# Eight linear-attention layers rewritten: centred weights, the residual added by TensorE, split f32r products, unrolled

## The chip, the cores and the metric

The kernel runs on one core of one Trainium2 chip. The metric is the time of one execution in device microseconds. All inputs are float32; the whole network is one launch.

## The reference, cut to what matters

The program chains six parts over an activation x of 4 sequences of 512 tokens with 128 features: a mixture of experts with 8 experts (A), a stack of eight linear-attention layers (B), part A again, an attention part with 4 experts (C), a state-space part (D), and C again. Only B is changed. Its input is the normalized x, and its output is added to x. One layer, with H = 16 heads of DH = 8 features and F = 512:

```python
def _phi(t):
    return jax.nn.elu(t) + 1.0

def layer(h, p):
    q = _phi((h @ wq + bq_).reshape(b, s, H, DH))
    k = _phi((h @ wk + bk_).reshape(b, s, H, DH))
    v = (h @ wv + bv_).reshape(b, s, H, DH)
    kv = jnp.einsum('bshd,bshm->bhdm', k, v)
    z = 1.0 / (jnp.einsum('bshd,bhd->bsh', q, k.sum(axis=1)) + 1e-06)
    att = jnp.einsum('bshd,bhdm,bsh->bshm', q, kv, z).reshape(b, s, d)
    h = h + att @ wo + bo_
    h = _ln(h, g1_, be1_)
    y = jax.nn.gelu(h @ w1 + c1_, approximate=False) @ w2 + c2_
    return (_ln(h + y, g2_, be2_), None)
```

After eight layers a last normalization with its own scale and shift follows, `_ln(h, gf, bef)`. `_ln` subtracts the mean over the 128 features and divides by the root of the variance.

## The kernel before

The activation lies with features on the 128 partitions and tokens along the free dimension, as four tiles of 128x512, one per sequence (batch b). Every engine has its own instruction list, written out by hand in program order, and waits on named semaphores; there is no planner. PSUM has 8 banks of 128x512.

Stage B is `pe_layers` (L646), `act_layers` (L719), `dve_layers` (L750) and `sp_layers` (L805); GpSimd (POOL) has no work in it. On each engine a loop of four iterations holds two layers, one for each half of the weight buffer `wslot`. SyncE loads the 901.5 KB of a layer's weights when the layer two before it has been left.

One layer goes so. Queries (L657): one fp32 product per batch, exponential and relu on ACT (L729, L730), minimum and sum on DVE (L761). Keys and values (L664): products of 256 columns for each 128 tokens, bias added by DVE (L774, L775), exponential and relu on ACT (L734, L735), DVE again (L767). DVE takes keys(b-2) after the bias of batch b, so keys lag by two batches. Then k times v with an extra column for the sum of keys (L672), masked by head on DVE (L784, L785), the denominators (L678), `rz` with the small constant on ACT (L737), its reciprocal on DVE (L788), the numerator product (L684) copied by ACT (L740), the spread of the reciprocal over heads (L688), the multiplication (L792), and the output projection (L692). DVE adds bias and residual (L796).

A normalization is `pe_ln`, `act_ln` and `dve_ln`: a mean product (L225, a matrix of 1/128), DVE subtracts it (L248), ACT squares (L234), a second mean product gives the variance (L228), ACT takes the logarithm (L242) and the exponential of minus half of it (L238), and DVE scales (L260) and shifts (L253). The feed-forward part has 16 fp32 products for 4 batches and 4 chunks of 128 hidden features (L701), 16 gelus (L746), 16 products back (L708), and DVE's bias and residual add (L801). PE issues ff1(b) and then ff2(b-1). A second normalization ends the layer. ACT loads its table for gelu before the first gelu, and the table with logarithm and exponential for each normalization.

The expert stages, which aren't changed, already split an fp32 operand into a high part in the type f32r and a low part, the difference, and add three products, high by high, low by high and high by low: L440, L441 and L442. There the weights' high part is a cast on DVE (L543) and the low part a subtraction on POOL (L526). Their hidden tiles are rounded by ACT (L495) and subtracted by DVE (L548). POOL also adds expert outputs (L519). In the state-space part DVE does a scan (L1439) and POOL a product (L1456).

Of the kernel before, what the change touches and what calls it, by code (L numbers as in the profile page):

```python
# [28 lines left out]
B_WQ, B_WKV, B_WO, B_W1, B_W2, B_KVB, B_VEC = 0, 128, 384, 512, 1024, 1536, 1792  # L29
B_BQ, B_BO, B_C1, B_C2, B_G1, B_BE1, B_G2, B_BE2, B_COLS = (B_VEC + i for i in (0, 1, 2, 6, 7, 8, 9, 10, 11))  # L30
# [8 lines left out]
    ("b_bc", 1), ("w_dt", DT_RANK), ("b_dt", 1), ("w_dtp", P), ("b_dtp", 1), ("a_log", NSTATE), ("dcoef", 1),  # L39
]  # L40

CONSTS = [("ident", P), ("mean", P), ("block", P), ("head_sum", 32), ("head_spread", P),
# [12 lines left out]
def build(nc, x_in, pack_a, pack_b, pack_c, params, consts, out, stages="ABACDC"):  # L55
    par_at, par_cols = columns(PARAMS)
    con_at, con_cols = columns(CONSTS)
    with ExitStack() as ctx:
# [47 lines left out]
        def view16(at, *shape):  # L106
# [30 lines left out]
        kv_bd, ks_h = view(10368, NB, P), view(10880, NB, 32)  # L137
        hid_b = view(11392, 2, FC, SEQ)
        k_exp, k_relu = view(0, NB, TPB, P), view(2048, NB, TPB, P)
        rz, att = view(0, SEQ), view(2048, NB, SEQ)  # L140
# [33 lines left out]
            gated_ok added gv_mm silu_ok q_mm q_act qf_ok kv_mm kv_ok k_act kf_ok kvs_mm kvbd_ok den_mm  # L174
            den_ok att_mm num_ok rz_ok z_bc att_ok o_mm res1_ok ff1_mm gelu_ok ff2_mm res2_ok x_ok conv_all
# [4 lines left out]
            a_exp a_ok diag_ok rows_clear bb_mm b_free cb_mm cc_ok da_ok scan_ok  # L180
# [10 lines left out]
        for kind in stages:  # L191
# [9 lines left out]
            elif kind == "B":  # L201
                count["ln"] += 2 + 2 * LAYERS
                count["lns"] += 1 + 2 * LAYERS
                count["w"] += LAYERS
                count["x_upd"] += 1
# [438 lines left out]
        ATT_BANK = [5, 6, 7, 4]  # L644

        def pe_layers(pe, c):  # L646
            n0 = c["ln"] + 1
            with pe.Fori(0, LAYERS // 2) as r:
                l = 2 * r
                for s in range(2):  # L650
                    m = 4 * (l + s)
                    w = wslot[:, s, :]
                    nd = n0 + 2 * (l + s)
                    pe.wait_ge(S[f"w_in{s}"], w_count(c, l))
                    for b in range(NB):
                        pe.wait_ge(S["ln_out"], 4 * nd - 4 + b + 1)
                        pe.matmul(ps[:, b, :], w[:, B_WQ:B_WQ + P], ha[:, b, :], start=True,  # L657
                                  stop=True).then_inc(S["q_mm"], 1)
                    for b in range(NB):
                        bank = 4 + 2 * (b % 2)  # L660
                        if b >= 2:
                            pe.wait_ge(S["kv_ok"], m + b - 2 + 1)
# [87 lines left out]
        def dve_layers(dve, c):  # L750
            n0, m0 = c["ln"] + 1, c["lns"]
            with dve.Fori(0, LAYERS // 2) as r:
                l = 2 * r
                for s in range(2):
# [15 lines left out]
                    for b in range(NB):  # L770
# [6 lines left out]
                        if b >= 2:  # L777
                            keys(b - 2)
# [948 lines left out]
```

## Time and profile before

| | us |
|---|---|
| median of 3 runs | 2228.36 (2226.25 to 2234.08) |
| the profiled execution | 2234.25 |
| its span, first to last instruction | 2232.5 |
| PE busy in the span | 1889.7 (85%) |
| DVE busy | 1437.7 (64%) |
| ACT busy | 1330.7 (60%) |
| POOL busy | 533.2 (24%) |

Times are microseconds, a count is written with x. PE is the matrix engine, PEld its weight load; a product of fp32 operands is recorded as two instructions. The granted clock of PE is a share of full speed: 1.00 is 2.4 GHz, 0.50 is 1.2 GHz. The mean over the span was 0.929. Lines of a view name the kernel's line, the engine, the operation, and the output and input tensors; `arena` is a large buffer that many tensors share. A duration is from the start of an instruction to its end, so it holds the time in which the instruction stands for a port or in a pipeline, and instructions of one engine can overlap a little.

### The profile page before, as it was taken

The page shows a single profiled execution, that of the slowest core. Times are in us where ns is not written, and L with a number is a line of the kernel's source. Part 1 is how long each engine was busy: PE and PEld are TensorE (multiplying, and loading weights), DVE is VectorE, ACT ScalarE, POOL GpSimd, SP SyncE. Part 2 cuts the span into 40 slices and gives each one's busy share as a digit, 9 for nine tenths or more (in the row PEclk, how much of TensorE's full clock was granted, in tenths as well). Part 3 has the DMA queues.
Part 4 walks back from the last instruction along what each step waited for, and adds up shares of the span by engine and source line. Part 5 has one row for each costly group of instructions (what it writes and reads, how often), then busy time and mean ns, then how long its engine had stood idle before and what let it go on. Part 6 is the DMA issues. An engine that isn't in the chain of part 4 may idle for free.

```text
span 2232.5 us, 23751 instructions
## 1 busy us (share of the span) xinstructions
PE 1889.7 (85%) x8305; PEld 1065.8 (48%) x8324; DVE 1437.7 (64%) x2318; ACT 1330.7 (60%) x2118; POOL 533.2 (24%) x525
## 2 busy tenths in 40 slices
PE   8899999999999989899677777997677677777998
PEld 6687444444434437686223233784122222332686
DVE  6687554465445646786755563786899755653787
ACT  6698646465555558797355556555654545565554
POOL 1344000000000001444411113122499501113121
PEclk9899999999999999899779998998799868999899
DMA  2431000000000003321000000210000000000110
GB/s 72 81 76 51 15 17 17 0 17 17 17 0 17 9 10 57 69 69 44 1 1 1 1 1 1 72 34 0 9 4 30 1 1 1 1 1 1 48 57 19
DMA packets 60610, 52.39 MB, mean 23 GB/s; under 512 B 2336, under 2 KB 55968, under 8 KB 60512
## 3 DMA queue, kind: packets, MB, share of 16 engines
q1 hardware_dynamic: 60512, 51.12, 8.9%
q8 instruction: 57, 0.93, 0.2%
q14 instruction: 41, 0.34, 0.1%
HBM read 49.47 MB, written 1.64 MB: 23 GB/s over the span
## 4 chain that ended last, share of the span: by engine, by line
PE 54%; DVE 22%; ACT 15%; issue 5%; DMA 2%; POOL 1%; SPq 0%; ACTq 0%; DVEq 0%; POOLq 0%
PE ps L440 8%; PE ps L442 8%; PE ps L441 8%; PE ps L708 5%; DVE arena L1439 4%; PE ps L225 4%; DVE arena L1184 4%; PE ps L701 4%; PE ps L927 3%; ACT arena L1047 2%; PE ps L897 2%; ACT rstd L242 2%; ACT arena L997 2%; ACT rstd L238 2%; PE ps L886 2%
## 5 line engine op out<-in xcount | busy, mean ns | idle before, releaser
L548 DVE TENSOR_TENSOR hid_lo<-arena,hid_hi 128x512 fp32r<-128x512 f32 x384 | 340.0, 897 | 72.2 <-ACT arena L498 70.2
L1184 DVE TENSOR_REDUCE arena<-ps 128x1 f32<-128x512 f32 (+3 forms) x352 | 214.0, 639 | 90.2 <-PE ps L901 87.4
L526 POOL TENSOR_TENSOR w_lo<-wslot,w_hi 128x512 fp32r<-128x512 f32 x56 | 76.7, 1374 | 787.8 <-DVE w_hi L543 787.8
L1104 POOL TENSOR_SCALAR_AFFINE_SELECT arena<-arena 128x256 f32<-128x256 f32 x256 | 102.5, 406 | 465.4 <-ACT arena L1047 462.8
L440 PE MATMUL ps<-x_hi,w_hi 128*128 128x512 f32 x512 | 208.7, 408 | 2.9 <-POOL w_lo L526 2.2
L441 PE MATMUL ps<-x_lo,w_hi 128*128 128x512 f32 x512 | 205.5, 401 | 0.0
L442 PE MATMUL ps<-x_hi,w_lo 128*128 128x512 f32 x512 | 205.2, 401 | 0.0
L495 ACT ACTIVATE hid_hi<-ps,wslot 128x512 fp32r<-128x512 f32 x256 | 177.1, 692 | 44.9 <-PE ps L442 17.7
L1047 ACT ACTIVATE arena<-ps 128x1024 f32<-128x1024 f32 (+3 forms) x256 | 166.3, 705 | 46.6 <-PE ps L917 45.9
L897 PE MATMUL ps<-arena 128*128 128x128 bf16 (+3 forms) x498 | 134.2, 336 | 63.5 <-DVE arena L1184 35.8
L498 ACT ACTIVATE arena<-ps,wslot 128x512 f32<-128x512 f32 x256 | 175.1, 684 | 16.8 <-DVE hid_lo L548 16.8
L440 PE MATMUL ps<-hid_hi,w_hi 128*128 128x512 f32 x384 | 153.4, 400 | 20.5 <-DVE hid_lo L548 20.5
L997 ACT ACTIVATE arena<-ps 128x1024 bf16<-128x1024 bf16 x64 | 65.4, 1021 | 151.0 <-PE ps L886 150.9
L442 PE MATMUL ps<-hid_hi,w_lo 128*128 128x512 f32 x384 | 152.9, 398 | 0.0
L441 PE MATMUL ps<-hid_lo,w_hi 128*128 128x512 f32 x384 | 151.8, 395 | 0.0
L1456 POOL TENSOR_TENSOR arena<-arena 128x512 f32<-128x512 f32 x64 | 136.1, 2165 | 45.8 <-ACT arena L1381 45.8
L519 POOL TENSOR_TENSOR x<-x,arena 128x512 f32<-128x512 f32 x64 | 108.2, 1694 | 149.6 <-DVE arena L510 149.6
L611 ACT ACTIVATE arena<-ps 128x512 f32<-128x512 f32 x128 | 76.3, 596 | 110.6 <-PE ps L442 110.5
L234 ACT ACTIVATE sq<-xc 128x512 f32<-128x512 f32 x92 | 57.6, 630 | 141.1 <-DVE xc L248 141.0
L801 DVE SCALAR_TENSOR_TENSOR res<-ps,wslot,hb 128x512 f32<-128x512 f32 x32 | 24.0, 751 | 182.7 <-PE ps L708 182.7
L701 PE MATMUL ps<-hb,wslot 128*128 128x512 f32 x256 | 116.7, 599 | 10.1 <-ACT arena L746 5.6
L746 ACT ACTIVATE arena<-ps,wslot 128x512 f32<-128x512 f32 x128 | 83.6, 690 | 67.7 <-PE ps L701 67.3
(223 smaller groups left out, 3876.7 us busy)
## 6 DMA issues: line engine op xcount, KB each, us to landing
arena<-gates_dram SPq DMA_DIRECT2D x96, 256.0 KB, 5.1
wslot<-pack_a SPq DMA_DIRECT2D x16, 514.5 KB, 3.6
wslot<-pack_b SPq DMA_DIRECT2D x8, 901.5 KB, 4.6
wslot<-pack_c SPq DMA_DIRECT2D x8, 768.0 KB, 4.6
res<-x_in SPq DMA_DIRECT2D x4, 256.0 KB, 4.4
out_dram<-res SPq DMA_DIRECT2D x4, 256.0 KB, 2.8
bc_dram<-arena SPq DMA_DIRECT2D x1, 384.0 KB, 3.2
arena<-bc_dram SPq DMA_DIRECT2D x16, 24.0 KB
```

The source lines that it names most:

```text
L440: pe.matmul(ps[:, bank, :], w1, hi, start=start, stop=False)
L441: pe.matmul(ps[:, bank, :], w1, lo, start=False, stop=False)
L442: return pe.matmul(ps[:, bank, :], w2, hi, start=False, stop=stop)
L495: act.activation(hid_hi[item % 2][:, k, :], ps[:, k, :], ACT.Gelu, bias=bias)
L498: act.activation(hid32[:, k, :], ps[:, k, :], ACT.Gelu, bias=bias).then_inc(S["hi_ok"], 1)
L548: dve.tensor_tensor(hid_lo[item % 2][:, k, :], hid32[:, k, :], hid_hi[item % 2][:, k, :].bitcast(F32), ALU.subtract).then_inc(S["hid_ok"], 1)
L701: pe.matmul(ps[:, k, :], w[:, B_W1 + k * P:B_W1 + (k + 1) * P], hb[:, b, :], start=True, stop=True).then_inc(S["ff1_mm"], 1)
L708: mm = pe.matmul(ps[:, 4 + b, :], w[:, B_W2 + k * P:B_W2 + (k + 1) * P], hid_b[:, b % 2, k, :], start=(k == 0), stop=(k == FC - 1))
L897: pe.matmul(ps[:, bank, m * keys:(m + 1) * keys], qt_s[h % 2][:, h // 2, i * P:(i + 1) * P], kt_s[b % 2][:, h // 2, 0:keys], start=(m == 0 ...
L1047: act.activation(pt[:, u % NPT, :, 0:n], ps[:, 2 * r:2 * r + 2, 0:n], ACT.Exp, scale=SCALE).then_inc(S["exp_ok"], 1)
L1184: dve.tensor_reduce(neg_max[:, i, heads[0]:heads[-1] + 1:step], ps[:, bank, 0:len(heads) * keys].rearrange("p (m k) -> p m k", k=keys), AX ...
L1456: pool.tensor_tensor(ch[:, s, t, :], hst[:, s, t, :], c_s[:, u % 2, :], ALU.mult).then_inc(S["ch_ok"], 1)
```

## The change

For each layer, and in program order:

- DVE prepares the next layer's weights during the feed-forward part: it sums the 128 output columns of Wo and of the four blocks of W2 (a reduction over 640 columns), subtracts the mean (one operation of 640 columns), and casts 640 columns (Wq, W1) and 512 columns (W2) to f32r. POOL subtracts to get the low parts.
- The constant `cent`, identity minus 1/128, is multiplied by the high and low parts of h on PE, into the same PSUM bank as the projection with the centred weights. So the bank holds the centred sum of residual and projection, and there is no mean product and no residual add. The bias, centred once for all layers, is given with the square and with the scaling.
- `kv_bd` is transposed and multiplied by the centred Wo on PE, copied back by ACT, and the queries are multiplied by the spread reciprocal before one product with it. The product of the numerator, and its copy, go. Denominators are packed into 256 columns in place of 512.
- Queries, ff1 and ff2 use three f32r products. ACT writes the high part of each normalized tile with an Identity operation; the low part is a subtraction on DVE for the middle of the layer and on POOL for h. The gelu's output is written in fp32 by ACT, copied to f32r by DVE, and subtracted on POOL; each ff2 chunk waits for both.
- ff1 and ff2 alternate by chunk, with three banks for ff1. The second normalization of batches 0 to 2 stands within and right behind the feed-forward part; that of batch 3 between the queries of the next layer. The keys(b) operation follows keys_values(b) with less lag.
- The loops are unrolled. The ACT table with logarithm and exponential is loaded once per layer, by hand, behind the gelus.

The diff, cut to its core:

```diff
 def pe_layers(pe, c):
+    def split3(bank, w_at, s, hi, lo, lo_ready, stop, start=False):
+        w1, w2 = (t[s][:, w_at:w_at + P] for t in (wb_hi, w_lo))
+        pe.matmul(ps[:, bank, :], w1, hi, start=start, stop=False)
+        pe.matmul(ps[:, bank, :], w2, hi, start=False, stop=False)
+        lo_ready()
+        return pe.matmul(ps[:, bank, :], w1, lo, start=False, stop=stop)
+    def centred(bank, hi, lo, stop):
+        pe.matmul(ps[:, bank, :], cent_r[:, :], hi, start=True, stop=False)
+        return pe.matmul(ps[:, bank, :], cent_r[:, :], lo, start=False, stop=stop)
-    with pe.Fori(0, LAYERS // 2) as r:
+    for l in range(LAYERS):
+        pe.wait_ge(S["w_parts"], c["parts"] + 2 * l + 2)
+        queries(0)
+        if l:
+            last_var(j1 - 1)
+        keys_values(0); queries(1); queries(2); keys_values(1)
+        queries(3); keys_values(2); keys_values(3)
...
+        for b in range(NB):
+            pe.wait_ge(S["g_ok"], m + b + 1)
+            centred(b, h_hi[:, b, :], h_lo[:, b, :], False)
+        pe.wait_ge(S["rz_ok"], l + 1)
...
+            pe.wait_ge(S["qz_ok"], m + b + 1)
+            pe.matmul(ps[:, b, :], kv_bd[:, b, :], qf[:, b, :], start=False, stop=True)
+        for b in range(NB):
+            var(j1, b, 4 + b)
...
+        def ff2(b, k):
+            if k == 0:
+                centred(4 + b, mid_hi[:, b, :], mid_lo[:, b, :], False)
+            pe.wait_ge(S["gelu_hi"], 16 * l + FC * b + k + 1)
+            mm = split3(4 + b, B_W2 + k * P, s, hb_b[b % 2][:, k, :], lb_b[b % 2][:, k, :],
+                        lambda: pe.wait_ge(S["gelu_lo"], 16 * l + FC * b + k + 1), k == FC - 1)
+        for item in range(NB + 1):
+            for k in range(FC):
+                if item < NB: ff1(item, k)
+                if item: ff2(item - 1, k)
...
 def act_layers(act, c):
+        queries(0)
+        if l: root(j1 - 1, 3, LN2_BANK[3])
+        queries(1)
+        if l: high(j1 - 1, 3, h_hi, ...)
+        queries(2); keys(0); queries(3); keys(1); keys(2); keys(3)
...
+        for b in range(NB):
+            root(j1, b, 4 + b)
+            if b: high(j1, b - 1, mid_hi, g1, be1, S["mid_hi_ok"])
...
 def dve_layers(dve, c):
+        queries(0)
+        if l: scaled(j1 - 1, 3, ...); shifted(j1 - 1, 3, ...)
+        queries(1); keys_values(0); queries(2); keys(0); keys_values(1)
+        queries(3); keys(1); keys_values(2); keys(2); keys_values(3); keys(3)
...
+                dve.wait_ge(S["gelu_ok"], n + 1)
+                dve.tensor_copy(hb_b[b % 2][:, k, :], hid_g[:, b % 2, k, :]).then_inc(S["gelu_hi"], 1)
+                if l + 1 < LAYERS and b in (1, 2) and k in (1, 3):
+                    weights(l + 1, 2 * (b - 1) + k // 2)
...
+def pool_layers(pool, c):
+            for b in range(NB):
+                low(l, b)                       # h_lo = ha - h_hi
+            for b in range(NB):
+                for k in range(FC):
+                    pool.wait_ge(S["gelu_hi"], 16 * l + FC * b + k + 1)
+                    pool.tensor_tensor(lb_b[b % 2][:, k, :], hid_g[:, b % 2, k, :],
+                                       hb_b[b % 2][:, k, :].bitcast(F32), ALU.subtract)
+                    if l + 1 < LAYERS and b == 3 and k in (0, 2):
+                        weights(l + 1, k // 2)
```

## Rows read from the trace of the kernel before

**Rows 1.** Busy time by stretch: stretch, length, PE, PEld, DVE, ACT, POOL, PEclk, DMA, GB/s.
```profile
232.20:813.30 581.10, 540.56 (x1601) 259.61 (x1601) 306.23 (x487) 330.74 (x514) 0.00 (x0) 1.00 0.03 11
```
**Rows 2.** Chain that ended last, parts of one layer: start, duration, what.
```profile
610.29 2.95 PE ps L672 x24
...
615.58 3.36 DVE arena L788
...
620.88 3.70 PE ps L692 x8
...
635.67 0.70 ACT arena L746
...
650.41 3.43 PE ps L701 x8
...
660.71 3.45 PE ps L225 x8
```
**Rows 3.** Timeline of PE: f32r products at half and at full clock; start, duration.
```profile
1399.33 0.63 PE L440 MATMUL ps<-x_hi,w_hi 128*128 128x512 f32 x1
1399.75 0.63 PE L441 MATMUL ps<-x_lo,w_hi 128*128 128x512 f32 x1
...
1403.18 0.39 PE L440 MATMUL ps<-x_hi,w_hi 128*128 128x512 f32 x1
1403.41 0.39 PE L441 MATMUL ps<-x_lo,w_hi 128*128 128x512 f32 x1
```
**Rows 4.** Timeline of ACT: logarithms of two batches with two operations between them.
```profile
837.80 0.67 ACT L279 ACTIVATE rstd<-ps,con 128x512 f32<-128x512 f32 x1
...
839.55 0.67 ACT L279 ACTIVATE rstd<-ps,con 128x512 f32<-128x512 f32 x1
```
**Rows 5.** Timeline of DVE and of POOL, in two stages where both work.
```profile
146.17 0.69 DVE L548 TENSOR_TENSOR hid_lo<-arena,hid_hi 128x512 fp32r<-128x512 f32 x1
146.78 1.52 DVE L543 CAST w_hi<-wslot 128x512 fp32r<-128x512 f32 x1
...
148.88 1.33 DVE L548 TENSOR_TENSOR hid_lo<-arena,hid_hi 128x512 fp32r<-128x512 f32 x1
...
146.31 1.71 POOL L526 TENSOR_TENSOR w_lo<-wslot,w_hi 128x512 fp32r<-128x512 f32 x1 [2.43 <-DVE w_hi L543]
148.38 1.29 POOL L526 TENSOR_TENSOR w_lo<-wslot,w_hi 128x512 fp32r<-128x512 f32 x1 [0.36 <-DVE w_hi L543]
...
1618.04 23.66 POOL L1456 TENSOR_TENSOR arena<-arena 128x512 f32<-128x512 f32 x11
```
**Rows 6.** Timeline of one layer: keys and values on PE, DVE and ACT.
```profile
600.24 3.62 PE L664 MATMUL ps<-wslot,ha 128*128 128x256 f32 x16
...
606.55 0.69 DVE L774 TENSOR_TENSOR arena<-ps,wslot 128x512 f32<-128x512 f32 x1 [0.89 <-PE ps L664]
...
608.41 0.61 ACT L735 ACTIVATE arena<-arena 128x512 f32<-128x512 f32 x1
...
609.55 1.99 DVE L767 SCALAR_TENSOR_TENSOR arena<-arena 128x512 f32<-128x512 f32 x3
```
**Rows 7.** Busy time by stretch, two in the attention stage, one in the state-space stage.
```profile
1197.20:1200.60 3.40, 1.69 (x16) 0.58 (x16) 0.00 (x0) 3.10 (x6) 1.48 (x4) 0.95 0.00 0
1207.20:1213.50 6.30, 5.17 (x36) 2.79 (x34) 1.79 (x6) 4.86 (x9) 1.31 (x4) 0.50 0.00 0
1620.00:1640.00 20.00, 14.41 (x37) 4.73 (x38) 20.00 (x19) 9.83 (x13) 20.00 (x11) 1.00 0.01 4
```
**Rows 8.** Timeline at the two ends of stage B.
```profile
232.16 4.84 PE L657 MATMUL ps<-ha,wslot 128*128 128x512 f32 x8
...
235.78 0.07 DVE L1611 MEMSET arena<- 128x16 f32 x1
...
826.15 2.49 DVE L1617 TENSOR_TENSOR x<-x,hb 128x512 f32<-128x512 f32 x4
```

More of the change, by code:

```diff
@@ L201, in build @@
             elif kind == "B":
-                count["ln"] += 2 + 2 * LAYERS
-                count["lns"] += 1 + 2 * LAYERS
+                count["ln"] += 1
                 count["w"] += LAYERS
+                count["parts"] += 2 * LAYERS
                 count["x_upd"] += 1
@@ L805, in sp_layers @@
[L805 to L816 removed]
+            n0 = 4 * c["ln"]
@@ new lines, in final_add, with weights, low @@
+        def final_add(dve, b):
+            dve.wait_ge(S["mid_hi_ok"], 4 * LAYERS + b + 1)
+            dve.tensor_tensor(x[:, b, :], x[:, b, :], hb[:, b, :], ALU.add).then_inc(S["x_ok"], 1)
+        def pool_layers(pool, c):
+            n0 = 4 * c["ln"]
+            def weights(l, cut):
+                s, (a, b) = l % 2, CUTS[cut]
+                pool.wait_ge(S["w_hi_ok"], c["parts"] + 2 * l + cut + 1)
+                pool.tensor_tensor(w_lo[s][:, a:b], wslot[:, s, a:b], wb_hi[s][:, a:b].bitcast(F32),
+                                   ALU.subtract).then_inc(S["w_parts"], 1)
+            def low(l, b):
+                if l:
+                    pool.wait_ge(S["h_ok"], 4 * l - 4 + b + 1)
+                else:
+                    pool.wait_ge(S["ln_out"], n0 + b + 1)
+                pool.wait_ge(S["h_hi_ok"], 4 * l + b + 1)
+                pool.tensor_tensor(h_lo[:, b, :], ha[:, b, :], h_hi[:, b, :].bitcast(F32),
+                                   ALU.subtract).then_inc(S["h_lo_ok"], 1)
+            for cut in range(2):
+                weights(0, cut)
+            for l in range(LAYERS):
+                for b in range(NB):
+                    low(l, b)
+                for b in range(NB):
+                    for k in range(FC):
+                        pool.wait_ge(S["gelu_hi"], 16 * l + FC * b + k + 1)
+                        pool.tensor_tensor(lb_b[b % 2][:, k, :], hid_g[:, b % 2, k, :],
+                                           hb_b[b % 2][:, k, :].bitcast(F32), ALU.subtract).then_inc(S["gelu_lo"], 1)
+                        if l + 1 < LAYERS and b == 3 and k in (0, 2):
+                            weights(l + 1, k // 2)
+            for b in range(NB):
+                low(LAYERS, b)
@@ L823, in build @@
+        def sp_layers(sp, c, slot_free):
+            for l in range(LAYERS):
+                s = l % 2
+                if l < 2:
+                    slot_free(sp, s)
+                else:
+                    sp.wait_ge(S["h_hi_ok"], 4 * l)
+                    sp.wait_ge(S["h_ok"], 4 * l - 4)
+                sp.dma_start(wslot[:, s, 0:B_COLS], pack_b[l]).then_inc(S[f"w_in{s}"], 16)
         SCALE = DH ** -0.5
@@ L1535, in _ @@
                     pe_layers(pe, c)
-                    last = n + 2 * LAYERS
-                    pe_ln(pe, last + 1, ha, lambda pe, t: pe.wait_ge(S["ln_out"], 4 * last + t + 1))
                 elif kind == "C":
@@ L1557, in _ @@
                     pool_experts(pool, c, x, EXPERTS0, A_PIECES, GATE_LAG0)
+                elif kind == "B":
+                    pool_layers(pool, c)
                 elif kind == "C":
```

492 lines of the change are left out of this document (316 added, 176 removed).

## The prediction

> **What bounds the kernel now.** I read the table by stretches first: the eight layers take 581.1 us of the 2232.5 us span, 72.64 us each, with PE busy 540.6 us, the granted clock at 1.00 throughout and POOL unused [rows 1]. So PE is nearly full, and removing PE work looks attractive: but the end of a layer is set by a chain, which I read next. One layer of it, with these marks [rows 2]: the first output-projection product runs to 621.74 (start 620.88 plus a quarter of 3.70); the first gelu starts at 635.67; the second feed-forward products end at 660.71; the k-times-v products end at 613.24, that is 685.88 one layer later; the next first projection ends 694.38. Four sections then make the layer: A, projection to gelu, 13.9; B, gelu to end of feed-forward, 25.0; C, that end to the end of the key-value products, 25.2; D, denominators, reciprocal, spread, first projection, 8.5. Sum 72.6. Within B the chain stands on PE all the time; in C and D it changes between ACT, DVE and PE.
>
> **What the change takes from PE.** An fp32 product of 512 columns is two passes of 0.43 us (8 passes in 3.43 us, the x8 rows) [rows 2]. An f32r product costs 0.23 at full clock and 0.43 at half [rows 3]. Three of them are 0.69 against 0.86. Per layer: 32 feed-forward products save 5.4, 4 queries 0.7, the 8 mean products 6.9, the 4 numerator products 3.4; added are 16 centring products, 3.7, and small transposes and weight products, about 1.3. PE falls from 67.6 to about 56 us. None of this is worth anything by itself; it must be followed through the sections.
>
> **Section A.** The mean product, DVE's subtraction and the residual add go (the centred sum stands in PSUM); squares start right behind the projections. The four variances wait for the last projection, so the first is there 3.6 us after the mark. Then ACT: logarithm and exponential take 1.24 per batch; with the new fourth operation (the high part) in between, 1.75, as the row pair in an expert stage shows [rows 4]. First exponential at 4.9, then three turns of 1.75 to 10.2, the last high part waiting for DVE's scaling to 11.1, table load 1.3: gelu starts 12.4 after the mark. A is 12.4, a gain of 1.5. The other table load, hidden in D before, goes at no gain.
>
> **Section B.** Each of 16 gelu tiles is now copied by DVE (f32r high part) and subtracted by POOL (low part), before the three ff2 products. The rows show how these two work beside each other: a POOL subtraction alone takes 1.29 us, beside a DVE operation that started first 1.71. A DVE cast that needs about 0.43 takes 1.52 when it meets a POOL operation: begun at 146.78, it ends at 148.30, 0.28 behind POOL's end at 148.02; a DVE subtraction takes 1.33 for the same reason; and a scan and a POOL product run alternately, 11 POOL products in 23.66, 2.15 each [rows 5]. So cast and subtraction take turns: 1.29 + 0.28 + 0.08 = 1.65 per tile when the cast waits each time, 1.17 + 0.28 = 1.45 when POOL is always queued (1.17 is 148.02 minus the DVE end 146.86). I take 1.55. B is then 1.2 (gelu 0.7, cast 0.4), 15 x 1.55 + 1.3 = 24.6, the next layer's weights, and the last ff2 product 0.4. Weights: POOL splits 640 and 512 columns, 1.46 + 1.17; DVE's centring operation of 640 columns and two casts hold POOL for 0.7 + 0.35 + 0.3, its three shifts for 0.3 each: 4.9, of which I count 4.4, since a cast fits ahead of a POOL weight operation. B comes to 30.6, a loss of 5.6. PE has 24.3 us of work in this section after the first three products, so it isn't the bound. Bounds: 28.5 at 1.45, 32.5 at 1.65, 40 if the turn is the 2.15 of the scan row, 27 if POOL never waits (then PE at 24.3 plus start and end). A gelu-table Square might force loads between gelus: four of 1.28 a layer, in ACT time that is only one third used here; zero to 5, I take zero.
>
> The Trainium skill (SBUF — State Buffer, "Who interferes with whom") says that DVE in a two-port mode, or with two SBUF inputs, and a GpSimd operation that reads SBUF exclude each other: the one that issues first keeps the pair for its whole instruction. The 1.52 and 1.33 rows agree [rows 5]. Without that rule one would add only POOL's own 16 operations, and B would be the 27 of the last bound.
>
> **Section C.** The normalization of batches 0 to 2 is now done under the feed-forward tail; only batch 3 is late, and it is passed by the next queries. The cost is a new tail: POOL's low part of h (1.3) stands behind its last gelu subtraction, so queries(0) end 1.3 after the mark, last variance 2.1, keys/values(0) 3.95 (8 passes of 3.62/16 = 0.23 [rows 6]). ACT does queries(0), root(3), queries(1), high(3), queries(2) in that order; DVE comes to keys/values(0) at 6.7. From there DVE and ACT hand each key batch back and forth. Before, the order lagged keys by two batches; now keys(1), kv(2), keys(2), kv(3), keys(3) follow without lag. One such turn is read from batch 2 of before: DVE starts at 606.55, ACT ends 608.41 + 0.61 = 609.02, and a DVE operation takes 0.68 more (1.99 for three, overlapping): 3.15 us [rows 6]. I follow it: kv(1) ends 11.1, keys(1) 13.1, kv(2) 14.3, keys(2) 16.25, kv(3) 17.45, keys(3) 19.45, the products of batch 3 end 20.6. C falls from 25.2 to 20.6, a gain of 4.6. Bounds: 17 if PE alone set it, 22 if DVE meets POOL's four low parts each time.
>
> **Section D.** Masks and transpose 1.1, denominators 0.5, reciprocal of half the columns 1.75 for 3.35 [rows 2], spread and multiply 2.0, projection 0.9, the PE queue's centring ahead of the spread 0.6: 6.9, a gain of 1.6. Bounds 6 and 8.
>
> Sum: 12.4 + 30.6 + 20.6 + 6.9 = 70.5, before the clock.
>
> **The clock.** PE has new holes. In C it has nothing from 15.1 to 16.3 and from 17.3 to 19.5 after the mark; in A it does three split products and then waits 3.4 us for the first gelu; at B's end it waits for POOL between single tiles. The rows: in 3.40 us with PE busy 1.69 the clock began to fall (mean 0.95), and 6.30 us behind another hole of that attention stage ran wholly at 0.50; where PE works 14.4 of 20 us in short regular pieces it kept 1.00 [rows 7]. The hole in C is sparser than the first of these. I expect a fall there in nearly every layer; at half clock the key-value, denominator, centring and projection products double, of which 1 to 4 us are on the chain: 2.3. In A the four tiles of lead absorb most: 0.5. At B's end the fall comes only sometimes: 0.7. Total 3.5, bounds 0 and 8. The layer is 74.0, against 72.64: plus 1.4.
>
> **Ends of the stage.** Before layer 0 the weights are split with nothing to hide it: LN done 235.8, DVE reduce, centre, two casts to 238.4, POOL 239.9 and 241.1, low part 242.4, while the queries started at 232.16 before [rows 8]. At half clock, after that wait, the keys/values of batch 0 then reach DVE at 249.2, the first projection ends about 271 instead of 258.2: plus 13 (bounds 8 and 15). Seven full layers follow: 7 x 1.4 = 9.8. The last A and B are 12.4 + 30.6 + 0.5 for 38.9: plus 4.6. The closing normalization starts from a finished centred sum; after the last ff2 product I count 16.3 + 1.2 for the clock, against 22.6 (x complete at 828.6 [rows 8]): minus 5. Loads of weights stay hidden, their DMA being asked for a full section B ahead. Unrolling is taken at nothing: the loop's branches aren't on the chain with more than issue time of a few tenths, so at most 0.5 us a layer is to be had; a price for fetching the longer code is in no row, and the unrolled expert stages show none on their chain.
>
> Sum: 13 + 9.8 + 4.6 - 5 = plus 22.4. The profiled execution took 2234.25 us (span 2232.5), 6 above the median 2228.4 of the three runs; plus 22 on the median gives 2250 us, slower by 1.0%.
>
> **The rivals.**
> 1. *The clock stays at 1.00.* Place: sections C and A; price 3.5 a layer, 4 at the start. For it: all layers now show 1.00 [rows 1]. Against: their gaps are below 1 us. It gives 9 - 7 x 2.1 + 4 - 6 = -8: 2220 us, not slower. It decides if the hole before the last key-value product leaves the clock alone.
> 2. *POOL isn't in the way.* If casts get ahead of POOL and their waits fall between its operations, B is 27.5, bounded by PE, and the layer with clock costs 71: 13 - 11.5 + 1.5 - 5 = -2; with the full clock as well, -32: 2226 and 2196. The point at which it turns: a tile turn under about 1.4 us. Against: the 1.52 cast.
> 3. *POOL's turn is 2.15, as beside the scan.* B is 9 longer in eight layers: plus 94, 2322 us. For it: [rows 5]; against: the scan holds DVE far longer than a cast.
>
> **How the numbers follow.** Forecast 0.45; rival 1 0.2; rival 2 0.17 (both parts); rival 3 0.06; 0.12 for milder mixtures on either side. Less than 0.3% (7 us) from 2228 is what a measurement of this kernel can't tell from no change. The forecast's own range is 2232 to 2280, almost all of it slower. Rival 1 is half in "faster", rival 2 half clearly faster, mixtures half: faster 0.33, same 0.12, slower 0.55. The range takes in rival 1, most of rival 2 and the upper unknowns without rival 3: 2195 to 2300.
>
> **What would show it.** The gelu subtractions on POOL should come every 1.45 to 1.65 us, filling the feed-forward stretch, with DVE casts of over 1 us; B should be 28 to 33 us. Keys of the last batch should end about 19.5 us after the last ff2 product, in turns of 3.15. The clock should show pieces at 0.50 around the key-value products. Queries of layer 0 should start near 242. Subtractions faster than 1.4, a head below 19, or a clock of 1.00 in all layers would make the prediction wrong on the side of faster; gelu table loads within the feed-forward part, on the other.

## The result, and the profile after

The changed kernel took 2259.56 us (median of 4 runs, 2258.0 to 2263.28) beside 2228.69 us for the kernel before on the same chip: a ratio of 1.0138, 95% interval 1.0115 to 1.0160. It is slower by 31 us; the forecast was 22 more, 2250. Its profiled execution took 2258.0 us with a span of 2256.3, 23.8 above the 2232.5 of before. The traces thus show 24 of the 31 us: the profiled execution of the kernel before lay 5.6 above the median of its runs, that of the changed kernel 1.6 below.

The first view is the table by stretches of the changed kernel: first the stage from its first product to its last feed-forward product (the stretch that answers to [rows 1]), then sections B, C, D and A of the layer around 600 us. Sections run here from start to start of the four marks: first output-projection product, first gelu, last feed-forward product, last key-value product. Columns: stretch, length, busy time of PE, PEld, DVE, ACT, POOL, granted clock, DMA share, GB/s.

```profile
238.16:833.41 595.25, 499.01 (x2048) 338.89 (x2048) 394.11 (x544) 361.25 (x592) 245.68 (x174) 0.95 0.03 11
584.03:612.64 28.61, 26.48 (x100) 19.78 (x100) 23.47 (x24) 18.08 (x28) 25.94 (x19) 0.94 0.00 1
612.64:633.40 20.76, 15.81 (x80) 12.52 (x80) 14.79 (x27) 13.32 (x23) 5.31 (x4) 1.00 0.13 46
633.40:644.67 11.27, 10.53 (x55) 5.34 (x52) 2.94 (x5) 2.48 (x9) 0.00 (x0) 0.85 0.00 0
644.67:658.69 14.02, 9.75 (x25) 4.48 (x25) 9.23 (x15) 11.90 (x18) 0.00 (x0) 1.00 0.00 0
```

PE was relieved as meant, from 540.6 us busy in 581 to 499.0 in 595, part of that at a lower clock; DVE now has 394 us and POOL 246. The same marks give these means over the seven layers from one first output-projection product to the next. B is 26.95 in the last layer, which has no next weights to split, and D is 11.9 in the first. (The expectations below take means over all eight layers, B 28.4 and D 10.9.)

| section, us | before | after | difference | forecast without clock |
|---|---|---|---|---|
| A | 14.8 | 14.0 | -0.8 | -1.5 |
| B | 24.45 | 28.6 | +4.2 | +5.6 |
| C | 25.4 | 20.8 | -4.6 | -4.6 |
| D | 7.9 | 10.8 | +2.9 | -1.6 |
| clock | | (in the rows above) | | +3.5 |
| a layer | 72.57 | 74.24 | +1.67 | +1.4 |

The second view is the chain that ended last, parts of one layer [rows 2]: start, duration, what.

```profile
612.55 1.49 POOL h_lo L1037
...
625.40 0.69 DVE arena L953
...
628.51 0.69 DVE arena L953
...
631.61 0.70 DVE arena L953
632.36 1.16 PE ps L721 x8
633.64 0.99 PE ps L731 x2
634.63 0.85 PE ps L732 x2
...
637.65 0.55 PE ps L731 x2
638.20 0.43 PE ps L732 x2
...
644.67 3.70 PE ps L752 x8
```

Two things are to be seen. Keys follow each other in turns of 3.11 (625.40, 628.51, 631.61), the 3.15 read from [rows 6]. And behind the key-value products PE itself is the chain: for each of four batches a product of the denominators in two halves (L731, L732), two passes each, with a transposition ahead of each (L729). At full clock that is 0.55 + 0.43 + 0.26 = 1.24 a batch, nearly 5 us in all.

The third view is the timeline of POOL and DVE in section B of that layer, which answers to [rows 5].

```profile
586.91 10.39 POOL L1048 TENSOR_TENSOR lb_b<-arena,hb_b 128x512 fp32r<-128x512 f32 x7 [0.36 <-DVE hb_b L1003]
...
605.50 1.76 POOL L1028 TENSOR_TENSOR w_lo<-wslot,wb_hi 128x640 fp32r<-128x640 f32 x1
607.22 2.70 POOL L1048 TENSOR_TENSOR lb_b<-arena,hb_b 128x512 fp32r<-128x512 f32 x2
609.88 1.30 POOL L1028 TENSOR_TENSOR w_lo<-wslot,wb_hi 128x512 fp32r<-128x512 f32 x1
611.13 1.47 POOL L1048 TENSOR_TENSOR lb_b<-arena,hb_b 128x512 fp32r<-128x512 f32 x1
```
```profile
584.75 0.43 DVE L1003 CAST hb_b<-arena 128x512 fp32r<-128x512 f32 x1 [1.10 <-ACT arena L873]
...
596.08 1.84 DVE L1003 CAST hb_b<-arena 128x512 fp32r<-128x512 f32 x2
597.83 1.58 DVE L916 CAST wb_hi<-wslot 128x640 fp32r<-128x640 f32 x1
```

The first cast, with POOL idle, takes 0.43. The other casts of this stretch take between 0.41 and 1.52 (mean over the stage 0.996), and the subtractions start 1.44 apart (median of the steps; seven end within 10.39). POOL has no gap longer than 0.4 us up to its last operation; the last feed-forward product starts at 612.64, as that ends. This is the turn that the prediction took from the 1.52 row. The Trainium skill (SBUF — State Buffer, "Who interferes with whom") has the same rule, one of the two holding the shared ports for its whole instruction; the casts of 0.43 beside an idle POOL and of up to 1.52 beside a busy one agree with it.

The rest is three pairs of rows. PE at the border of A and B; DVE and PE at the start of the stage; DVE's last additions to x.

```profile
584.77 0.50 PE L661 MATMUL ps<-mid_hi,w_hi 128*128 128x512 f32 x1 [3.67 <-ACT arena L873]
...
586.31 0.63 PE L664 MATMUL ps<-mid_lo,w_hi 128*128 128x512 f32 x1
```
```profile
235.36 1.56 DVE L929 CAST cent_r<-con 128x128 fp32r<-128x128 f32 x1
...
238.16 0.77 PE L661 MATMUL ps<-h_hi,w_hi 128*128 128x512 f32 x1 [8.80 <-POOL w_lo L1028]
```
```profile
849.80 0.69 DVE L1020 TENSOR_TENSOR x<-x,hb 128x512 f32<-128x512 f32 x1
...
851.74 0.69 DVE L1020 TENSOR_TENSOR x<-x,hb 128x512 f32<-128x512 f32 x1
```

PE waits 3.67 us for the first gelu; some eight of its next products then run at a clock of 0.50. This is so in seven of the eight layers; layer 1 kept 1.00 throughout section B. At the start a cast of 128 columns took 1.56 beside POOL. From the last feed-forward product to the last addition to x there are 21.8 us, against 23.4 before [rows 8].

The balance of the two spans: the stage is entered 2.8 earlier (DVE's last step of the first normalization starts at 232.30 for 235.12, in code that wasn't changed); from there to the first output-projection product 17.5 more; seven layer periods 11.7 more; the last A and B 1.7 more; the closing 1.6 less; what follows 2.85 less, in code that wasn't changed. Sum 23.7, of 23.8. The unchanged part after the stage took 1394.6 to 1405.2 us in the profiled executions of the twelve kernels that have the changed stage, so a few us there mean nothing.

### The profile page after: what moved, and what is told of

Read it like the earlier page. It is cut to its first block, busy times and chain, and to the rows that moved or that the text cites. A ratio compares the mean times of both kernels' runs of the same rounds, so it can differ in the third digit from the quotient of the medians.

```text
span 2256.3 us, 24548 instructions
## 1 busy us (share of the span) xinstructions
PE 1849.1 (82%) x8774; PEld 1141.6 (51%) x8774; DVE 1527.1 (68%) x2377; ACT 1372.2 (61%) x2213; POOL 786.6 (35%) x705
## 4 chain that ended last, share of the span: by engine, by line
PE 48%; DVE 25%; ACT 14%; issue 6%; POOL 4%; DMA 3%; SPq 0%; POOLq 0%; DVEq 0%; ACTq 0%
PE ps L449 7%; PE ps L451 7%; PE ps L450 7%; DVE arena L1682 4%; DVE arena L1427 4%; PE ps L1170 3%; PE ps L1140 3%; ACT arena L1290 2%; ACT arena L1240 2%; PE ps L234 2%; PE ps L1129 2%; DVE hb_b L1003 2%; PE ps L1160 1%; POOL lb_b L1048 1%; DMA arena<-gates_dram 1%
## 5 line engine op out<-in xcount | busy, mean ns | idle before, releaser
L1048 POOL TENSOR_TENSOR lb_b<-arena,hb_b 128x512 fp32r<-128x512 f32 x128 | 182.7, 1450 | 324.4 <-DVE hb_b L1003 324.4
L1140 PE MATMUL ps<-arena 128*128 128x512 bf16 (+3 forms) x512 | 139.5, 339 | 63.6 <-DVE arena L1427 34.5
L1003 DVE CAST hb_b<-arena 128x512 fp32r<-128x512 f32 x128 | 123.9, 996 | 30.2 <-ACT arena L873 29.7
L1140 PEld LDWEIGHTS ps<-arena 128*128 128x128 bf16 x512 | 43.0, 102 | 161.5 <-DVE arena L1427 99.8
```

The costliest lines, as they stand in the source:

```text
L1003: dve.tensor_copy(hb_b[b % 2][:, k, :], hid_g[:, b % 2, k, :]).then_inc(S["gelu_hi"], 1)
L1048: pool.tensor_tensor(lb_b[b % 2][:, k, :], hid_g[:, b % 2, k, :], hb_b[b % 2][:, k, :].bitcast(F32), ALU.subtract).then_inc(S["gelu_lo"], 1)
L1140: pe.matmul(ps[:, bank, m * keys:(m + 1) * keys], qt_s[h % 2][:, h // 2, i * P:(i + 1) * P], kt_s[b % 2][:, h // 2, 0:keys], start=(m == 0 ...
```

## The experiments

Every ratio is against the kernel before, run on the same chip in turn; the changed kernel itself is 1.0138. Dummy products write a PSUM bank that the next product overwrites.

**e1: the clock.** Twelve more products fill PE's holes in section C.

```diff
 # pe_layers, behind the four key-value products of batch b
+for _ in range({1: 4, 2: 8}.get(b, 0)):
+    pe.matmul(ps[:, 3, :], cent_r[:, :], h_hi[:, 0, :], start=True, stop=True)
```

> The changed kernel with 4 and 8 f32r products without use (into bank 3, overwritten later) in PE's two holes before the key-value products of batches 2 and 3; nothing else. Sections, from start marks (first projection product, first gelu, last ff2 product, last key-value product) of the changed kernel: A 14.0, B 28.4, C 20.8, D 10.9 us, and D is 9.9 in the two layers in which the clock is at 1.00 there. Theory (the fall of the clock in the hole costs only what D shows): D about 9.9 in every layer, 1.1 x 8 = 9 us less, 2250. Rival (the forecast's price, 3.5 us a layer from the clock): 28 us less, about 2232. If the holes have nothing to do with the clock: no change, or slower by what the products displace.

Measured: 2252.28, ratio 1.0093 (1.0067 to 1.0119). Section D was 9.9 with the clock at 1.00 in all layers, C 20.7, the period 73.44 against 74.24. In the changed kernel D swings from 9.9 at 1.00 to 11.5 at 0.85, with a mean of 10.8. So D costs 2.0 more than before (7.9) even at full clock, and the fall of the clock in D 0.9 a layer: about a quarter of the forecast 3.5. The time alone doesn't show it, as the interval of the ratio touches that of the changed kernel; the period does.

**e2: the order of the denominators.** All first halves, then all second halves, then the transpositions, so that neighbours write different groups of 32 partitions of PSUM; ACT copies the denominators first.

```diff
 for b in range(NB):
     pe.wait_ge(S["kvbd_ok"], m + b + 1)
-    pe.transpose(ps[:, b, 256:256 + P], kv_bd[:, b, :], ident).then_inc(S["kvt_mm"], 1)
-    rows = ps[32 * b:32 * b + 32, 4, 0:256]
-    pe.matmul(rows, ks_h[:, b, 16:48], qf[:, b, 0:256], start=True, stop=False, ...)
-    mm = pe.matmul(rows, ks_h[:, b, 0:32], qf[:, b, 256:512], start=False, stop=True, ...)
+    pe.matmul(ps[32 * b:32 * b + 32, 4, 0:256], ks_h[:, b, 16:48], qf[:, b, 0:256], ...)
+for b in range(NB):
+    mm = pe.matmul(ps[32 * b:32 * b + 32, 4, 0:256], ks_h[:, b, 0:32], qf[:, b, 256:512], ...)
 mm.then_inc(S["den_mm"], 1)
+for b in range(NB):
+    pe.transpose(ps[:, b, 256:256 + P], kv_bd[:, b, :], ident).then_inc(S["kvt_mm"], 1)
```

> The changed kernel with the denominators of all four batches issued first (first halves, then second halves) and the four transposes behind them; ACT writes rz before it copies the transposes. In the changed kernel these 12 products take 5.0 to 6.2 us one behind the other (about 1.24 per batch at full clock), where four denominator products of 512 columns took 1.6 together before. Theory (the interleaved transposes keep the four batches from overlapping, and that is the mis-sized term of D): D from 10.9 to 8, 23 us less, about 2236. Rival (D is set by the reciprocal chain and the clock): under 6 us less.

Measured: 2237.84, ratio 1.0026 (1.0008 to 1.0044); D 8.5 at a clock of 0.80, period 71.69. This edit alone took back 2.55 us a layer. The products show as follows, all at full clock: PE in the kernel before, which I had not followed closely enough; the changed kernel; then e6, which has the order of e2. The first line of each is a window that ends within 0.3 us of its first product, so its count tells how many had started by then.

```profile
685.73 0.63 PE L678 MATMUL ps<-arena 128*32 128x512 f32 x3
685.73 1.66 PE L678 MATMUL ps<-arena 128*32 128x512 f32 x8
```
```profile
637.58 0.40 PE L731 MATMUL ps<-arena 128*32 128x256 f32 x1
637.58 0.62 PE L731 MATMUL ps<-arena 128*32 128x256 f32 x2
```
```profile
667.77 0.42 PE L729 MATMUL ps<-arena 128*32 128x256 f32 x3
667.77 1.00 PE L729 MATMUL ps<-arena 128*32 128x256 f32 x7
...
669.35 0.66 PE L736 MATMUL ps<-con,arena 128*128 128x128 f32 x4
670.15 1.16 PE L739 MATMUL ps<-wslot,kv_t 128*128 128x128 f32 x8
```

Each is recorded with 32 columns of weights, and batch b writes the group of partitions from 32b on. In the kernel before three passes, each about 0.6 long in the record, start within 0.02 us and are done in 0.63: passes for different groups run side by side, and eight of 512 columns take 1.66, 0.21 each. In the changed kernel the four passes of a batch write one group and start one behind the other, about 0.22 apart, though they are half as long; then a transposition follows. In e6 three passes start within 0.02 us again and are done in 0.42, and seven take 1.00. So the denominators of four batches take 1.58 there (667.77 to 669.35) in place of 4 x 0.98 = 3.9, which is 2.3 of the gain, and the transpositions a few tenths less than 4 x 0.26. From the key-value products to the next step (L739) there are 2.4 us (667.77 to 670.15) where the changed kernel takes 4.9. Whether it is the groups alone or also the transpositions between them that keep the batches of the changed kernel apart stays open: e2 moved both at once.

**e3: low parts off POOL.** DVE does the gelu's subtraction in place of POOL, right behind its cast.

```diff
 dve.tensor_copy(hb_b[b % 2][:, k, :], hid_g[:, b % 2, k, :]).then_inc(S["gelu_hi"], 1)
+dve.wait_ge(S["gelu_hi"], n + 1)
+dve.tensor_tensor(lb_b[b % 2][:, k, :], hid_g[:, b % 2, k, :], hb_b[...], ALU.subtract)
```

> The changed kernel with the subtraction of the gelu's low part on DVE, behind its cast, in place of POOL; POOL keeps the weights' and h's low parts. Theory (casts and POOL subtractions take turns on a shared port and set B): DVE needs about 1.05 us per tile, PE 1.37, so B falls from 28.4 to about 26 and is bounded by PE; with POOL's queue free, h's low part comes earlier and C loses up to 1: 8 x 3 = 24 us less, 2236. Rival (PE or the order of ff1 and ff2 already sets B): under 5 us less. Second rival (DVE's own queue becomes the bound): no gain or slower.

Measured: 2258.98, ratio 1.0124 (1.0097 to 1.0151). B fell to 26.85 and C rose to 22.3: together 49.2, against 49.4 before the edit. B did what the theory said, and the layer gained nothing by it: the period is 74.04 for 74.24. The chain of e3 is PE with three products a tile and a tail on ACT:

```profile
605.25 0.23 PE ps L662
605.48 0.25 PE ps L664
...
605.76 0.69 ACT arena L873
...
606.47 1.28 ACT L877
...
607.76 0.69 ACT sq L803
...
613.58 0.58 ACT sq L803
```

ACT's gelus follow PE, 6 x 0.23 = 1.39 a tile (ff1 and ff2 of one chunk), only 0.05 faster than POOL's turn; and behind the last gelu there are 7 us of ACT up to the square of the last batch (613.58). The statistics of that batch stand in PE's list ahead of the next layer's keys, so C waits for this tail. The path over POOL and the path over PE and ACT were tied. Two stretches show it, and they come back below: G, from the first gelu to the last, and T, from the last gelu to the last key-value product of the next layer. The figures are medians over the layers.

| | G | T |
|---|---|---|
| changed kernel | 21.6 | 27.7 |
| e3 | 21.6 | 27.45 |

Taking the low parts off POOL left G as it was and shortened T by 0.2.

**e4: the lag of the keys put back.** keys(b) one place later in DVE's list.

```diff
 queries(2)
-keys(0)
 keys_values(1)
+keys(0)
 queries(3)
-keys(1)
 keys_values(2)
+keys(1)
-keys(2)
 keys_values(3)
+keys(2)
 keys(3)
```

> The changed kernel with DVE's keys one batch behind keys_values again (kv1, keys0, queries3, kv2, keys1, kv3, keys2, keys3). Theory (the three turns of 3.15 us between DVE and ACT set section C): C from 20.8 to about 17.3, 8 x 3.5 = 28 us less, about 2232, and PE's holes get shorter, so D a little shorter too. Rival (PE or the clock sets C): under 6 us less.

Measured: 2225.35, ratio 0.9981 (0.9963 to 0.9999); C 17.47, D 9.9 with the clock at 1.00, period 70.02. The turns of 3.11 are gone and with them the falls of the clock in C and D: C is shorter by 3.3 (0.2 of it clock) and D by the 0.9 that e1 found.

**e5: full clock at the first gelus.** Thirteen dummy products in PE's wait of 3.67, with a wait for the first logarithm so that they start after the statistics.

```diff
 # pe_layers, behind ff1 of the first chunks
+if (item, k) == (0, 2):
+    pe.wait_ge(S["blog_ok"], 4 * j1 + 1)
+    for _ in range(13):
+        pe.matmul(ps[:, 4, :], cent_r[:, :], h_hi[:, 0, :], start=True, stop=True)
```

> The changed kernel with 13 f32r products without use (3.0 us, into bank 4) in PE's wait between the first three ff1 products of a layer and the fourth, where PE stands 3.66 us until the first gelu has been computed. Nothing else. Theory (this wait makes the clock fall, and the pieces at half clock delay the first gelus: the last layer's B is 26.9 with the fall and was 25.3 in the run e4, where the fall didn't come): B from 28.4 to about 26.8 in every layer with a clock of 1.00, 13 us less, about 2247. Rival (the lead of four tiles absorbs it, as forecast with 0.5 us a layer): under 4 us less.

Measured: 2260.23, ratio 1.0124 (1.0096 to 1.0152). The clock of B was 1.00 in all layers, and B stayed 28.8 in layers 0 to 6; only layer 7 went from 26.95 to 25.29. The theory fell but for that layer: where next weights are split, the half clock is hidden behind POOL and DVE. G fell from 21.6 to 20.0, and T rose from 27.7 to 29.5. The changed kernel had shown as much in its layer 1, where the clock was 1.00 throughout B: G was 20.1 there, T 29.3 and B 28.8.

**e6: e4 and e2 together.**

> The edits of e2 (denominators first) and e4 (keys one batch behind) together. Theory (two separate terms, C 17.4 and D; without the hole D keeps its clock): D 7.9 or less against 8.5 at a clock of 0.80, period 74.2 - 3.3 - 3.0 = 68, 50 us less than the changed kernel, about 2208 and faster than the kernel before. Rival (with shorter sections the clock falls elsewhere, or the two gains overlap): D stays at 8.5, about 2215 or more.

Measured: 2210.86, ratio 0.9898 (0.9869 to 0.9926); A 14.0, B 29.2, C 17.7, D 7.4, period 68.37. The clock was 1.00 in C and D and 0.89 in B, which is 0.6 longer than in the changed kernel.

**e7: the second feed-forward product back in fp32.** One product from the gelu's output and the centred weights in fp32, no cast and no subtraction (ff1 and the queries stay split).

```diff
-pe.wait_ge(S["gelu_hi"], 16 * l + FC * b + k + 1)
-mm = split3(4 + b, B_W2 + k * P, s, hb_b[b % 2][:, k, :], lb_b[b % 2][:, k, :], ...)
+pe.wait_ge(S["gelu_ok"], 16 * l + FC * b + k + 1)
+mm = pe.matmul(ps[:, 4 + b, :], w[:, B_W2 + k * P:B_W2 + (k + 1) * P], hid_g[:, b % 2, k, :],
+               start=False, stop=k == FC - 1)
```

> The changed kernel with the second feed-forward part in fp32: one product per tile (0.86 us) from gelu's fp32 output in place of three f32r products (0.69), so without the 16 casts on DVE and the 16 subtractions on POOL per layer, and without the split of W2. Theory as formed after e3 (PE's six f32r products, 1.40 us, and the DVE-POOL turn, 1.44, are tied): PE's tile becomes 1.54, B grows by 15 x 0.1 = 1.5 us, and the last tile comes without POOL's tail (last subtractions 612.6 against gelu 605.6 in one layer), so C loses nothing and B+C is within 1.5 us of 49.2 a layer: between 2248 and 2272. Rival (the turn on the port alone sets B, as forecast): B down by 2 or more a layer, 2243 or less.

Measured: 2272.14, ratio 1.0175 (1.0149 to 1.0201). Section B of one layer:

```profile
672.00:701.20 29.20, 28.45 (x84) 16.82 (x85) 3.80 (x6) 16.79 (x25) 1.56 (x1) 0.94 0.00 0
```

DVE and POOL are all but idle here (3.8 and 1.6) and B is no shorter, 29.6 on the mean of seven layers: PE is busy 28.45 of 29.20, at 0.86 + 0.69 = 1.55 a tile. Taking away the engine that I had called the bound gained nothing, but this edit also makes PE's own tile 0.17 longer, so that e3 is the cleaner test. C was 22.3: T was 27.5 to 28.2, not shorter than the 27.7 of the changed kernel, so what B no longer waits for behind the last gelu, C waits for. B and C together were 51.8, above the 50.7 that the theory allowed, and the time stood at the upper end of its range.

**e8: all of it on DVE.** e6 with e3's subtraction, the square of the last batch earlier on ACT, and the first layer's weights split within the first normalization (as in e10, below).

```diff
+square(j2, 3, 7, S["ff2_mm"], c2)
 root(j2, 2, LN2_BANK[2])
 high(j2, 1, h_hi, g2, be2, S["h_hi_ok"])
-square(j2, 3, 7, S["ff2_mm"], c2)
 high(j2, 2, h_hi, g2, be2, S["h_hi_ok"])
```

> Both edits of e6, the subtraction of the gelu's low part on DVE (e3), ACT's square of batch 3 ahead of the third logarithm, and layer 0's weights split by DVE between the two halves of the first normalization. Theory (in e3 B+C stayed at 49.3 because ACT's tail behind the last gelu - table load, square, three roots, two high parts, and only then the square of batch 3 - ended last): with the square moved, e3's 1.5 us come through, and the start of the stage gains 4: 8 x 1.5 + 4 = 16 us less than e6, about 2192. Rival (ACT's tail or DVE's queue holds batches 0 to 2 as late as before): only the 4 us of the start, about 2204.

Measured: 2203.06, ratio 0.9866 (0.9841 to 0.9891), the rival's number; B 28.05, C 18.7, in all layers alike. Together they are 46.8, against 46.9 in e6, and the period is 68.23 for 68.37: nearly all that e8 gained stands outside the layers, and the first output-projection product comes at 260.85 in place of 264.66.

**e9: e8 with e5's dummy products.**

> The kernel of e8 (low part of the gelu's output on VectorE, scores beside the queries, denominators first, first weights split early) with thirteen dummy products in TensorE's wait between the second projection's last statistics and the first log, as in e5. In e5 they lifted the clock to 1.00 and gave nothing in layers 0 to 6, and the reading was that the turn of VectorE and GpSimd with the next layer's weights ended last there. In e8 that turn is gone: its layers 0 to 7 all show 28.05 from gelu to last product at a clock of 0.88, no shorter in layer 7. Theory: TensorE's pace sets this stretch now, so the half clock shows: 13 products at 0.43 in place of 0.23 are 2.6 us in each of 8 layers; B 25.4 to 26.4 instead of 28.05, 8 x 1.7 to 2.6 = 13 to 21 us less, 2182 to 2190 us. Rival: ScalarE's tail behind the last gelu, tied to gelus that wait for VectorE's two instructions of a turn (1.23), takes the lead back: B stays within 0.5 of 28.05 and the time is 2199 to 2204.

Measured: 2182.77; B 25.25, C 18.7, period 65.43, with the clock at 1.00 in B, C and D. The theory held, with B a little below its range. (The kernel has no edit of "scores"; it is e8 with the dummy products, which start behind the first logarithm.)

**e10: the start of the stage.** e6 with `cent` cast and the first weights split and centred by DVE ahead of its last steps of the first normalization.

```diff
 # dve_ln of the first normalization, behind the subtraction of the mean
+if mid:
+    mid()          # cast of cent, casts, reduction and centring of layer 0's weights
 # dve_layers
-for step in range(4):
-    weights(0, step)
-dve.tensor_copy(cent_r[:, :], ccol("cent")).then_inc(S["cent_ok"], 1)
```

> The kernel of e6 (2210.9 us) with the split and the centring of the first layer's weights moved by themselves ahead of VectorE's last steps of the first normalization, GpSimd keeping the gelu's low parts. Theory: the start of the stage lost 17.5 us against the kernel before of which this move returns only what stood between the normalization's end and the first product: first product 238.6 to 234.5 and first output product 264.7 to 260.8 as in e8, 4 us less, 2207 us; the sections of a layer stay at A 14.0, B 29.0, C 17.7, D 7.4. Rival: the small difference of e8 to e6 (8 us) was all from here and nothing from VectorE's low parts: 2203 us.

Measured: 2207.54; B 29.1, C 17.7, D 7.4, period 68.22, as expected.

**e11: e10 with e5's dummy products.**

> The kernel of e10 (2207.5 us, the gelu's low parts on GpSimd) with the thirteen dummy products of e9. It is the fourth corner of a square: GpSimd without dummies 2207.5 (e10), VectorE without 2203.1 (e8), VectorE with 2182.8 (e9, section B 25.25). Theory: where GpSimd computes the low parts, its turn with VectorE, with the next layer's weights in it, ends last in layers 0 to 6, so the full clock gives nothing there and 1.7 to 2.5 us in layer 7 alone (no weights to split): B 29.0 in seven layers and 25.3 to 26.1 in the last, time 2203 to 2206. Rival: the full clock is worth its 2.6 us a layer whichever engine computes the low parts, and e5 was hidden by something else (keys without lag): B 26.4, time 2187.

Measured, as the square that the four make:

| low parts by | without dummies | with them |
|---|---|---|
| POOL | e10: 2207.54 (B 29.1, last layer 27.8; period 68.22) | e11: 2201.53 (B 28.8, last layer 25.3; period 68.38) |
| DVE | e8: 2203.06 (B 28.05; period 68.23) | e9: 2182.77 (B 25.25; period 65.43) |

The ratios are 0.9875 (0.9857 to 0.9892) for e10, 0.9866 (0.9842 to 0.9889) for e11, and 0.9768 (0.9751 to 0.9786) for e9. Each step alone is worth 4 to 6 us between the medians, 2 by the ratios, whose intervals overlap, and nothing in the period. Both together are worth 25 us, and 2.8 in the period. (DVE's row also has ACT's new order of the square, which wasn't run by itself. That square waits for the last product of B, so it can't be what shortens B.) The stretches G and T say which path ended last:

| | G | T |
|---|---|---|
| e10 | 22.5 | 24.3 |
| e8 | 22.8 | 24.0 |
| e11 | 20.0 | 26.1 to 27.9 |
| e9 | 20.0 | 24.0 |

The dummy products take 2.5 us from G with POOL and 2.8 with DVE. With DVE, T stays as it was and the whole gain comes through. With POOL, T rises by 1.9 in the four layers where the clock stays at 1.00 in C, and by 3.5 in the three where it falls there (C is 17.4 and 19.1). So most of what the dummy products save is lost to POOL's path, and the rest to a fall of the clock that e10 didn't have. B came as the theory of e11 had it; the time is 1.5 us below its range.

Section B of a middle layer in e9, then a middle layer and the last one in e11:

```profile
602.21:627.46 25.25, 24.63 (x102) 18.93 (x101) 22.34 (x39) 16.36 (x25) 3.14 (x2) 1.00 0.00 0
```
```profile
616.24:644.99 28.75, 25.31 (x102) 18.45 (x101) 27.25 (x26) 18.96 (x28) 26.08 (x19) 1.00 0.00 0
753.26:778.55 25.29, 24.65 (x101) 18.79 (x101) 20.54 (x19) 16.29 (x25) 22.57 (x16) 1.00 0.00 1
```

In e9 PE is busy 24.63 of 25.25 us, so PE bounds B, and its clock counts. In e11 DVE is busy 27.25 and POOL 26.08 of 28.75; in the last layer, with 16 subtractions and no weights, the same kernel needs 25.29. So it isn't the gelu's low parts by themselves that lengthen B (16 x 1.44 = 23.0 fits under PE's 24.6) but they and the next layer's weights on the same pair of engines. Splitting the weights elsewhere with POOL kept for the low parts wasn't tried. e10 against e6 moved the first output-projection product from 264.7 to 260.4, 4.3 us as expected; the times, 2207.5 and 2210.9, differ by 3.3, which ranges of 6 to 8 us don't show by themselves.

e9 is the fastest version: 2.3% less than before, and 3.7% less than the changed kernel by the two ratios.

## Why the prediction came out as it did

The total was near (2250 against 2259.6, well inside the range) and the direction right; but the terms of D and of the clock were wrong in opposite directions, and that the sum held is luck in good part.

- **A**, forecast -1.5, measured -0.8. Three turns of ACT were taken at 1.75 [rows 4]; in the changed kernel logarithms come 1.94 apart, since the high part takes 0.80:

```profile
650.52 0.67 ACT L807 ACTIVATE rstd<-ps,con 128x512 f32<-128x512 f32 x1
...
651.76 0.80 ACT L813 ACTIVATE mid_hi<-rstd,wslot 128x512 fp32r<-128x512 f32 x1
652.46 0.67 ACT L807 ACTIVATE rstd<-ps,con 128x512 f32<-128x512 f32 x1
```

  The row that I used had no scale and shift per partition. The Trainium skill (ScalarE: Activation LUTs, "What ACT_TABLE_LOAD costs") puts about 0.09 us on each such operand; the 0.80 of this operation, with two, and the 0.69 of a gelu, with one, agree.
- **B**, forecast +5.6 with 1.55 a tile, measured +4.2 with 1.44: 16 x 0.11 is about the difference. The weights' share was forecast 4.4; POOL's row shows 27.3 us from its first gelu operation to its last (585.26 to 612.55), of which 16 x 1.44 = 23.0, so 4.3. The mechanism was right. What fell short is the sentence that PE isn't the bound: its tile stood 0.05 behind, and with ACT's tail it ended C at the same time. For rival 2, POOL not in the way, the forecast had B at 27.5 and the layer 3 shorter than in its main line. e3 is that case: B was 26.85, and the layer was 0.2 shorter.
- **C**, forecast -4.6, measured -4.6, by the turn of 3.15 read from one batch of before. The new order was followed and priced rightly; e4 shows what it gives away against the old lag, 3.1 us a layer or 25 us in eight, of the 31 by which the change is slower.
- **D**, forecast -1.6, measured +2.9, or +2.0 at full clock: the step that failed. In the forecast's own marks D was to be 6.9 and is 10.7 at full clock. Masks, transposition and "denominators 0.5" were 1.6 together, and measured are 4.9. I had put a pass of 256 columns at half of one of 512, and had read that one as 0.21 where four groups ran side by side. ACT's copy of the denominators, 0.5, isn't in the sum. e2's order brings the 4.9 down to 1.6, but D in e6 is still 8.3 in these marks, half a us less than before and not 1.6: with the reciprocal earlier, PE's weight products and centring hold the spread back by 1.5 us behind it (671.71 to 673.18 in e6), where the forecast had 0.6.
- **The clock**, forecast 3.5 a layer, measured 0.9 in D (e1) and at most 0.2 in C; the half clock at the head of B was there in seven of eight layers and hidden but in the last (e5). The falls before the last key-value product came as forecast, but began in most layers only at D. Rival 1 wanted 1.00 in all layers; e1 gave that for C and D, and 2252 us, not 2220, since the term of D was wrong beneath it.
- **The start**, forecast +13, measured +17.5. Up to the keys of layer 0 the forecast held: the bias of batch 0 begins on DVE at 246.7; the forecast was 249.2, less the 2.8 of the earlier entry. The 258.2 that its end was held against is near the start of that projection before (258.06), whose end is 258.9. What came late is D once more: 11.9 in layer 0, against 7.9 before. The cast of `cent`, 1.56 beside POOL, ends at 236.92, ahead of the weights' low part that the first product waited for, so it isn't the cause. **The last layer**, forecast +4.6 for its A and B, measured +1.7: the sum gave it 4.4 us of next weights, which it doesn't have. **The closing**, forecast -5, measured -1.6: the additions to x come 1.94 apart, the same turn of ACT as in A, and the clock was 0.85 on the mean.

With D alone put right (+2.0) the forecast would have been 8 x 3.6 = 29 us higher, 2279; with the clock alone put right (0.9 in place of 3.5) 7 x 2.6 = 18 lower, 2232. Neither is nearer to 2259.6 than the 2250 was. With both it is 2261; A adds 5, B takes 10 and the last layer 3, the closing adds 3 and what is left of the start 1, which makes 2257. That is the 29 us that the stage itself lost, where the forecast had 22. The rest of the difference to 2259.6 lies outside the stage and in how the profiled executions lie to their medians.

## What to carry to other kernels

Before work is moved off the busiest engine, work out the time per tile of every path that ends together (here 1.39 on PE, 1.44 on POOL with DVE, and a tail on ACT): with paths tied, removing one gives next to nothing, and removing two together gave 25 us. A rewrite's loss can sit in its order: the places of `keys(b)` and of the denominators' products and transpositions cost 5.9 us a layer (74.24 to 68.37 in e6), and changing them made the slower kernel 1% faster than before. Price small products from rows of the same shape with the same neighbours: here a pass's share of the time was 0.21 for 512 columns only because passes for other groups ran beside it.

## What was not expected of the hardware

- Passes of fp32 products with 32 columns of weights that write different groups of 32 partitions ran side by side: three of 512 columns in 0.63 at full clock, three of 256 in 0.42 (e6). Those that write one group ran one behind the other: two of 256 columns in 0.62 (changed kernel).
- DVE casts and POOL subtractions in turns settled at 1.44 us a pair in the changed kernel, below the sum of what each takes alone, 0.43 + 1.29 = 1.72.
- Products that compute nothing made the program faster where PE's clock was on the path: the ratio fell from 1.0138 to 1.0093 in e1 (the intervals meet) and from 0.9866 to 0.9768 between e8 and e9 (they don't).
